# A third place for x in the shared-expert stage, earlier loads and gathers, and constant rows by a transfer in attention

## The chip, the cores and the metric

One core of a Trainium2 chip runs the whole program: TensorE (PE), VectorE (DVE), ScalarE (ACT), GpSimd (POOL) and SyncE (SP), which only issues transfers here. The metric is the device time in microseconds, the median of three runs. SP's transfers go through one hardware queue, those that POOL issues (gathers and scatters by an index) through another.

## The reference, cut to what matters

```python
x = x + long_convolution(ctx, layernorm(x))      # 2048 tokens of 512
x = x + bitlinear_ffn(layernorm(x))
x = x + cross_attention(layernorm(x), ctx)       # 16 heads, 8 batches of 256 tokens
h = layernorm(x)                                 # the layer that the change is in:
aff = sigmoid(h @ wa)                            # 16 routed experts
topk_p, topk_i = top_k(aff, 2)                   # 2 experts a token, shares normalised
routed = sum over the two of share * expert(h)
shared = expert_s0(h) + expert_s1(h)             # 2 experts that every token takes
x = x + h + shared + routed
# expert(h) = (gelu(h @ g + gb) * (h @ w1 + b1)) @ w2 + b2,   512 -> 256 -> 512
```

## The kernel before, in words

The program is a sequence of blocks, and all engines meet at the end of each. Three of them matter.

**Attention** (`stage_attention`) goes through steps (b, u): batch b of 8, pair u of heads of 8, one step being g = 8b + u. Each engine has its list of work written out for every step. PE transposes scores with a stationary operand `kb[b % 2]`: 96 rows of keys and 32 constant rows of which two are ones and the rest zeros. The constant rows of `kb[0]` are made in the block before. Those of `kb[1]` (`at_kb`) are made at step (0, 2) by two memsets on DVE (L1577, L1579), and the output bias is split there too into a high and a low bf16 part (L1582, L1584). PE needs the constant rows at g = 8 and the bias at step (2, 0). DVE's copies of the turned maxima (`qs`, L1590) stand behind all this in its queue, and PE's `transposed_scores` (L1678) waits for them.

**Router** (`stage_router`) is untouched by the change. It leaves x + h in HBM, called x below (`mid_rows`, 16 tiles of 128 tokens).

**Route and shared** (`stage_route_and_shared`) does two things at once. PE runs the two shared experts over six chunks i of 256 tokens (CN = 6): `up(i, 0)`, `down(i - 1)`, `up(i, 1)`, where an `up` is 24 matmuls into `ps_sg` and 24 into `ps_su`. DVE adds each `down` to x (`add_sums`, L2186), which frees the banks that the next `down` needs. x for chunk i lies in one of two places: `s_x` for even i, `e_yo` for odd i. SP loads it (`load_x`, L2079) and stores the sum back (`store_x`, L2083). Beside this, the 32 weight matrices of the routed experts (512 KB each, number n) are loaded in order by SP (`load_raw`, L2074), rounded to bf16 by ACT (L2296), and the rest is subtracted out by POOL for even n (`gate_lows`, L2136) and by DVE for odd n (`up_lows`, L2179). A load waits until the matrix that had its place is done with. SP's queue is in order, so that a load of x stands behind the loads of weights that are ahead of it in the list. The list gives chunk i the weights `LOADS[i]`: 7 to 9, 10 to 13, 14 to 19, 20 to 25, 26 to 29, 30 and 31. Numbers 28, 29 and 30 wait for `up_lows(10)`, `gate_lows(11)` and `up_lows(11)`, and 31 waits for `gate_lows(14)`.

The routing itself: DVE works out a slot for each token and share. POOL scatters 32 pieces into a table in HBM (L2140), four between two `gate_lows`, and SP loads the finished table (`s_table`, L2104) behind weight 29. PE turns it (`turn_table`, L2360) between `down(4)` and `up(5, 1)`. DVE makes of it the token numbers of 47 blocks, and POOL gathers the rows of the first two blocks into `e_rows` (L2154). This is the last thing in POOL's list, behind `gate_lows(15)`.

**Experts** (`stage_experts`) runs the 47 blocks of 128 slots and then the shared experts for the last two chunks. Its first matmuls (`ps_ex`, L2640) turn the rows gathered above, then come `ps_eg` and `ps_eu`.

## Time and profile before

| | before |
|---|---|
| median of 3 runs | 1229.19 us (1228.75 to 1229.37) |
| the profiled execution | 1229.41 us, its span 1227.5 us |
| PE busy, weight loads | 1076.3 us (88%), 807.1 us (66%) |
| DVE, ACT, POOL busy | 896.5 us, 715.6 us, 600.0 us |
| mean granted clock of TensorE | 0.929 of 2.4 GHz |
| mean transfer rate | 151 GB/s |

The span runs from the first to the last instruction. Around it lie 1.9 us. PE is busy most of the time, but no engine is so all the time, since the blocks differ: what an edit is worth shows in the place where it stands.

### The profile page before, as it was taken

Reading aid. Unit: us, or ns where it says so; the run is one execution under the profiler, and the core shown is the slowest. Engines: PE = TensorE matmul, PEld = TensorE weight load, DVE = VectorE, ACT = ScalarE, POOL = GpSimd, SP = SyncE. Lnnn points to the kernel's source line nnn. Section 1 sums busy time; section 2 is a strip of 40 time slices with the busy share of each in tenths; the row PEclk is TensorE's granted clock in tenths of the full one; section 3 lists DMA queues with packets and bytes.
Section 4 is the critical chain, followed back from the end, with each engine's and each line's share of the span. In section 5 each row is a group of like instructions: output and inputs, shape, how many; then the busy total and the mean of one; then the engine's idle time right before and its main releaser. Section 6 shows DMA issues by size and latency. Waiting matters only on the chain. (4 is left out here: it accounts for less than half of the span.)

```text
span 1227.5 us, 25636 instructions
## 1 busy us (share of the span) xinstructions
PE 1076.3 (88%) x9595; PEld 807.1 (66%) x9691; DVE 896.5 (73%) x1671; ACT 715.6 (58%) x1090; POOL 600.0 (49%) x586
## 2 busy tenths in 40 slices
PE   5799996768999799967899998698988599999995
PEld 4677775734554567736777776397756488888883
DVE  6389998977888798667788888488845555555538
ACT  4475772758888555646788877295533255544530
POOL 1444441635455322336788888322686255555520
PEclk9899998879999999968999999857989899999998
DMA  7484431033333312321222220098588377677789
GB/s 278 144 269 128 155 106 60 7 112 121 120 103 125 116 34 95 96 87 27 53 55 58 59 58 11 13 385 295 131 240 249 129 238 239 240 242 242 236 308 366
DMA packets 77872, 185.03 MB, mean 151 GB/s; under 512 B 10032, under 2 KB 12230, under 8 KB 76860
## 3 DMA queue, kind: packets, MB, share of 16 engines
q1 hardware_dynamic: 61468, 139.92, 34.0%
q0 software_dynamic: 8544, 24.68, 6.6%
q10 hardware_dynamic: 7744, 18.88, 5.1%
q8 instruction: 74, 1.21, 0.5%
q14 instruction: 42, 0.34, 0.1%
HBM read 130.06 MB, written 47.09 MB: 144 GB/s over the span
## 5 line engine op out<-in xcount | busy, mean ns | idle before, releaser
L384 PE MATMUL ps_y<-kv,toep 128*128 128x288 f32 x640 | 159.1, 411 | 6.7 <-POOL kv L368 6.0
L384 PEld LDWEIGHTS ps_y<-kv,toep 128*128 128x128 f32 x640 | 122.4, 192 | 42.8 <-DMA toep<-taps_padded 8.5
L1489 POOL TENSOR_TENSOR vw<-at_pf,kw 128x1024 bf16<-128x1024 f32 x64 | 136.5, 2133 | 2.7 <-ACT kw L1546 2.7
L368 POOL TENSOR_TENSOR kv<-kx 128x1024 f32<-128x1024 f32 x32 | 60.6, 1893 | 87.9 <-PE ps_y L384 38.3
L2443 POOL DMA_INDIRECT expert_results<-e_yo,target x47 | 70.1, 1492 | 56.9 <-ACT e_yo L2486 56.9
L1542 ACT ACTIVATE at_pf<-ps_st 128x1024 f32<-128x1024 f32 x64 | 65.4, 1022 | 46.4 <-PE ps_st L1678 43.0
L1596 DVE TENSOR_REDUCE at_negmax<-ps_s 128x4 f32<-128x1024 f32 x64 | 78.4, 1224 | 2.8 <-PE ps_s L1639 0.8
L999 PEld LDWEIGHTS ps_eg<-e_xT,e_w 128*128 128x128 bf16 x1128 | 67.8, 99 | 14.6 <-issue 2.5
L2540 DVE COPY e_w<-expert_weights 128x4096 bf16 x47 | 57.7, 1227 | 23.6 <-issue 23.6
L999 PE MATMUL ps_eg<-e_xT,e_w 128*128 128x128 bf16 x1128 | 71.9, 221 | 3.4 <-DVE e_xT L2547 3.4
L940 PE MATMUL ps_fH<-w1T,f_qaT 128*128 128x512 bf16 x253 | 62.3, 402 | 9.9 <-ACT f_h L835 8.8
L999 PE MATMUL ps_eu<-e_xT,e_w 128*128 128x128 bf16 x1128 | 70.9, 219 | 0.0
L1546 ACT ACTIVATE kw<-at_pf 128x1024 bf16<-128x1024 f32 x64 | 67.7, 1057 | 2.0
L2553 DVE SCALAR_TENSOR_TENSOR e_y<-ps_eu,e_bias,e_y 128x128 f32<-128x128 f32 x94 | 28.6, 346 | 54.0 <-PE ps_eu L999 53.2
L2438 POOL DMA_INDIRECT e_rows<-token_rows,token x45 | 43.5, 967 | 48.7 <-PE ps_ex L2640 42.6
L999 PEld LDWEIGHTS ps_eu<-e_xT,e_w 128*128 128x128 bf16 x1128 | 65.3, 98 | 0.0
L2502 ACT ACTIVATE e_xT<-ps_ex 128x512 bf16<-128x512 bf16 x47 | 28.1, 597 | 63.7 <-PE ps_ex L2640 63.7
L1590 DVE COPY qs<-ps_m 32x256 bf16<-32x256 bf16 x128 | 37.6, 294 | 33.9 <-PE ps_m L1651 30.8
L408 DVE TENSOR_TENSOR prod<-ps_y,qx 128x1024 f32<-128x1024 f32 x32 | 39.1, 1223 | 29.2 <-ACT ps_y L337 29.1
L964 PE MATMUL ps_fY<-w2T,f_qbT 128*128 128x512 bf16 x242 | 57.4, 387 | 2.4 <-DVE x_res L773 1.7
L940 PEld LDWEIGHTS ps_fH<-w1T,f_qaT 128*128 128x128 bf16 x256 | 25.9, 103 | 42.3 <-issue 15.2
L2495 ACT ACTIVATE e_y<-ps_eg,e_bias 128x128 f32<-128x128 f32 x94 | 29.4, 363 | 37.9 <-PE ps_eg L999 29.7
(446 smaller groups left out, 3164.1 us busy)
## 6 DMA issues: line engine op xcount, KB each, us to landing
e_parts<-down_parts SPq DMA_DIRECT2D x47, 512.0 KB
w_raw<-in_L_ffn_w ACTq DMA_DIRECT2D x32, 512.0 KB, 4.8
toep<-taps_padded SPq DMA_DIRECT2D x32, 256.0 KB, 3.5
f_draw<-in_L_ffn_rw SPq DMA_DIRECT2D x16, 512.0 KB
down_parts<-f_dparts SPq DMA_DIRECT2D x16, 512.0 KB
expert_weights<-expert_results SPq DMA_DIRECT2D x16, 512.0 KB, 11.0
x_res<-in_x SPq DMA_DIRECT2D x4, 1024.0 KB, 11.8
c_in<-in_ctx SPq DMA_DIRECT2D x4, 1024.0 KB, 7.8
```

What stands on the lines that cost most here:

```text
L368: pool.tensor_tensor(pairs[:, :, :, 0:HD0], x[:, :, 0:HD0].unsqueeze(2).broadcast_to([P, ROWS_N, WIDE, HD0]), partners(x, 0, 1, WIDE), ALU ...
L384: last = pe.matmul(y[:, l * B:(l + 1) * B, :, WIDE - 1:], toep[h % 2][:, (DC - 1 - l + m) * P:(DC - l + m) * P], kv[h % 2][:, m * B:(m + 1 ...
L940: pe.matmul(psH[:, f, :], qaT[p][:, c, :], k.w1T[:, c * FF + f * 512:c * FF + (f + 1) * 512], start=(c == 0), stop=False)
L964: last = pe.matmul(psY[:, :], qbT[p][:, c, :], k.w2T[:, c * D:(c + 1) * D], start=(c == 0), stop=(c == FC - 1))
L999: instruction = pe.matmul(out, stationary[a], moving[b], start=first and n == 0, stop=last and n == 2)
L1489: pool.tensor_tensor(pl[u % 4][:, :, :, :], pf[u % 2][:, :, :, :], ph[u % 4][:, :, :, :], ALU.subtract)\
L1542: act.activation(pf[u % 2][:, :, :, :], psT[:, :, :, :], ACT.Exp, scale=SCORE_SCALE).then_inc(exped, 1)
L1546: act.activation(ph[u % 4][:, :, :, :], pf[u % 2][:, :, :, :], ACT.Copy).then_inc(p_high, 1)
L1596: dve.tensor_reduce(negmax[u % 2][:, :].rearrange("p (j q) -> p j q", j=2), psS[:, :, :, :], AX.X, ALU.max, negate=True).then_inc(max_read, 1)
L2438: pool.indirect_dma_start(out=rows[j % 2], out_offset=None, in_=k.scratch["rows"], in_offset=bass.IndirectOffsetOnAxis(ap=token[:, j:j + 1 ...
L2443: pool.indirect_dma_start(out=k.scratch["results"], out_offset=bass.IndirectOffsetOnAxis(ap=target[:, j:j + 1], axis=0), in_=yo[j % 2], in ...
L2540: dve.tensor_copy(w1[j % 2][:, :, :, :].rearrange("p h c f -> p (h c f)"), W[:, bass.ds(e, 1), :, :, :].rearrange("p o h c f -> p (o h c f ...
```

## The change

In the shared stage x has three places instead of two: `s_x`, `e_yo` and `e_rows` (the target of the later gathers), used in the order 0, 1, 2, 0, 2, 1. Each load has a semaphore for its place and half. The loads of chunks 0 to 2 are issued together near the start, that of chunk 3 ahead of weight 20, that of chunk 4 behind weight 29 and ahead of the table, and that of chunk 5 ahead of weight 30. A load into a used place waits for the store out of it, and each store waits for the store before it. PE turns the slot table between the two halves of the last `up`. POOL issues the two gathers ahead of `gate_lows(15)`, and each waits for the store of chunk 4 out of `e_rows`. In attention a transfer on SP copies the constant rows of `kb[0]` to `kb[1]` at the start of the block. The two memsets go, and the bias is split at step (1, 5).

```diff
@@ -1411,7 +1411,7 @@
             sem(n) for n in ("xn", "xtp", "xh", "xl", "qp", "sq", "no", "qh", "ql"))
         sum_psum, var_ready, r_ready, diag_ready, r_psum = (sem(n) for n in ("sup", "var", "rr", "di", "rp"))
         ot_psum, ot_high, ot_low, y_psum, y_added = (sem(n) for n in ("otp", "oth", "otl", "yp", "ya"))
-        maxes_high, ones_set, bias_zeroed, bias_high, bias_low, shift_ready = (sem(n) for n in ("mxh", "os", "bz", "bh", "bw", "xs"))
+        maxes_high, ones_copied, bias_zeroed, bias_high, bias_low, shift_ready = (sem(n) for n in ("mxh", "oc", "bz", "bh", "bw", "xs"))
         stacked, k_loaded = sem("st"), sem("kl")
         block = ctx.enter_context(nc.Block())
         G = UNITS
@@ -1433,6 +1433,7 @@
 
         @block.sync
         def _(sp):
+            sp.dma_start(kb[1][STACK:, :, :, :], kb[0][STACK:, :, :, :]).then_inc(ones_copied, 16)
             sp.wait_ge(bias_zeroed, 1)
             for row in (0, LO_ROW):
                 sp.dma_start(bo[row:row + 1, :], k.ins["L1_xattn_bo"].rearrange("(o d) -> o d", o=1)).then_inc(b_loaded, 16)
@@ -1573,10 +1574,7 @@
 
             for b, u in STEPS:
                 g = b * G + u
-                if b == 0 and u == 2:
-                    dve.memset(kb[1][STACK:, :, :, :], 0.0).then_inc(ones_set, 1)
-                    dve.wait_ge(ones_set, 1)
-                    dve.memset(kb[1][STACK:STACK + 2, :, :, :], 1.0).then_inc(ones_set, 1)
+                if b == 1 and u == 5:
                     lo_row = slice(LO_ROW, LO_ROW + 1)
                     dve.wait_ge(b_loaded, 32)
                     dve.tensor_copy(bo_parts[:, :], bo[:, :]).then_inc(bias_high, 1)
@@ -1671,7 +1669,7 @@
                 if g:
                     pe.wait_ge(exped, g)
                 if g == G:
-                    pe.wait_ge(ones_set, 2)
+                    pe.wait_ge(ones_copied, 16)
                 c, h0 = u // 2, 2 * (u % 2)
                 for j in range(2):
                     for kc in range(2):
@@ -1801,6 +1799,7 @@
 RAW_N = OWN_RAW + LENT_RAW
 SETS = 4
 LO_AT = 32
+X_PLACE = (0, 1, 2, 0, 2, 1)
 HI_AT = 64
 FRONT = 4
 K_ROWS = 96
@@ -2049,14 +2048,16 @@
         table_set, table_stored, table_loaded, table_turned = (sem(n) for n in ("tse", "tst", "tl", "tt"))
         cols_set, cols_ready, cols_turned, shares_ready, token_ready, rows_got = (sem(n) for n in ("cs", "cr", "ctn", "shr", "tok", "brow"))
         raw_loaded, raw_high, gate_low, up_low = [sem(f"rl{i}") for i in range(RAW_N + LENT_RAW)], sem("rh"), sem("gl"), sem("ul")
-        xT_loaded, x_loaded = ([sem(f"{n}{i}") for i in range(2)] for n in ("xtl", "xl"))
+        xT_loaded = [sem(f"xtl{i}") for i in range(2)]
+        x_loaded = [[sem(f"xl{i}{s}") for s in range(ST)] for i in range(max(X_PLACE) + 1)]
         block = ctx.enter_context(nc.Block())
         turned_dram = k.scratch["turned"].rearrange("(i s) p d -> i p s d", s=ST)
         mid_dram = k.scratch["mid"].rearrange("(t p) d -> t p d", p=P)
         table_dram = k.scratch["slots"]
         W_half = lambda n, h: W[:, n // 2, h, :, n % 2 * FE:(n % 2 + 1) * FE]
         rows_loaded, x_stored, late_loaded = fetched
-        x_tile = lambda i, s: e_yo[s] if i % 2 else x[:, s, :]
+        x_tile = lambda i, s: (x[:, s, :], e_yo[s], e_rows[s].bitcast(F32))[X_PLACE[i]]
+        x_uses = lambda i: [n for n in range(i + 1) if X_PLACE[n] == X_PLACE[i]]
         experts_of = lambda i: range(FIRST_E[i], FIRST_E[i + 1])
         shares_of = lambda tile: late_shares[0:K_ROWS, tile - ST * LATE[0], :] if tile // ST in LATE else (
             sharesT[0:K_ROWS, tile if tile < ST * LATE[0] else tile - 2 * ST, :])
@@ -2074,12 +2075,14 @@
                 sp.dma_start(raw_at(n), src).then_inc(raw_loaded[place_of(n)], 16)
 
             def load_x(i, s):
-                if i >= 2:
-                    sp.wait_ge(x_stored[s], 16 * (i - 1))
-                sp.dma_start(x_tile(i, s), mid_dram[EARLY[i] * ST + s, :, :]).then_inc(x_loaded[s], 16)
+                if len(x_uses(i)) > 1:
+                    sp.wait_ge(x_stored[s], 16 * (x_uses(i)[-2] + 1))
+                sp.dma_start(x_tile(i, s), mid_dram[EARLY[i] * ST + s, :, :]).then_inc(x_loaded[X_PLACE[i]][s], 16)
 
             def store_x(i, s):
                 sp.wait_ge(d_added, i * ST + s + 1)
+                if i:
+                    sp.wait_ge(x_stored[s], 16 * i)
                 sp.dma_start(mid_dram[EARLY[i] * ST + s, :, :], x_tile(i, s)).then_inc(x_stored[s], 16)
 
             for n in range(RAW_N):
@@ -2088,22 +2091,24 @@
             sp.dma_start(table_dram.rearrange("(j p) w -> j p w", p=BLK), table[:, :, :]).then_inc(table_stored, 16)
             sp.dma_start(bias_rows[0:E_N, 0:FE], k.ins["L1_ffn_rgb"]).then_inc(rows_got, 16)
             sp.dma_start(bias_rows[0:E_N, FE:], k.ins["L1_ffn_rb1"]).then_inc(rows_got, 16)
-            for s in range(ST):
-                load_x(0, s)
+            for i in range(3):
+                for s in range(ST):
+                    load_x(i, s)
             for i in range(CN):
-                for s in range(ST):
-                    if i >= 2:
-                        load_x(i - 1, s)
+                if i in (3, 5):
+                    for s in range(ST):
+                        load_x(i, s)
                 for n in LOADS[i]:
                     load_raw(n)
                     if n == LOADS[i][0] and i >= 2:
                         for s in range(ST):
                             store_x(i - 2, s)
+                if i == 4:
+                    for s in range(ST):
+                        load_x(i, s)
                 if i == CN - 2:
                     sp.wait_ge(scattered, 16 * 2 * NT)
                     sp.dma_start(table[:, :, :], table_dram.rearrange("(j p) w -> j p w", p=BLK)).then_inc(table_loaded, 16)
-            for s in range(ST):
-                load_x(CN - 1, s)
             for s in range(ST):
                 store_x(CN - 2, s)
             sp.wait_ge(gu_psum, (CN - 1) * SH_N)
@@ -2147,12 +2152,15 @@
             for e in range(2, E_N):
                 for n in range((e - 2) * 4, min((e - 1) * 4, 2 * NT)):
                     scatter(n)
-                gate_lows(e)
+                if e < E_N - 1:
+                    gate_lows(e)
             pool.wait_ge(scattered, 16 * 2 * NT)
             pool.wait_ge(token_ready, 1)
             for j in range(2):
+                pool.wait_ge(x_stored[j], 16 * (CN - 1))
                 pool.indirect_dma_start(out=e_rows[j], out_offset=None, in_=k.scratch["rows"],
                                         in_offset=bass.IndirectOffsetOnAxis(ap=token[:, j:j + 1], axis=0)).then_inc(rows_loaded[j], 16)
+            gate_lows(E_N - 1)
 
         @block.vector
         def _(dve):
@@ -2182,7 +2190,7 @@
             def add_sums(i):
                 for s in range(ST):
                     dve.wait_ge(d_psum, i * ST + (s + 1))
-                    dve.wait_ge(x_loaded[s], 16 * (i + 1))
+                    dve.wait_ge(x_loaded[X_PLACE[i]][s], 16 * len(x_uses(i)))
                     dve.tensor_tensor(x_tile(i, s), x_tile(i, s), psD[s][:, :], ALU.add).then_inc(d_added, 1)
 
             for t in range(NT):
@@ -2323,6 +2331,8 @@
         def _(pe):
             def up(i, p, e):
                 for ps, m in ((psG, 0), (psU, 1)):
+                    if m and i == CN - 1 and e == SH_N - 1:
+                        turn_table()
                     for f in range(F2):
                         for c in range(DC):
                             col = c * FE + f * P
@@ -2373,8 +2383,6 @@
                 pe.wait_ge(y_full, i * SH_N - 1)
                 up(i, i % 2, 0)
                 down(i - 1)
-                if i == CN - 1:
-                    turn_table()
                 pe.wait_ge(y_full, i * SH_N)
                 up(i, i % 2, 1)
             down(CN - 1)
```

## Rows read from the trace of the kernel before

**Rows 1.** Timeline, attention, 549 to 560 us: start, duration, engine, line, operation, [idle before it].

```profile
...
550.32 1.76 DVE L1577 MEMSET at_kb<- 32x2048 uint32 x1 [0.48 <-issue]
...
551.65 1.09 PE L1689 MATMUL ps_p<-ident,at_xn 128*128 128x128 f32 x4
...
552.99 3.47 DVE L1579 MEMSET at_kb<- 2x4096 bf16 x1 [0.91 <-DVE at_kb L1577]
556.49 0.42 DVE L1582 CAST at_bop<-at_bo 33x512 bf16<-33x512 f32 x1
556.95 0.68 DVE L1584 TENSOR_TENSOR at_bop<-at_bo,at_bop 1x512 bf16<-1x512 f32 x1
...
558.33 1.03 PE L1678 MATMUL ps_st<-qs,kb 128*128 128x256 bf16 x4 [5.58 <-DVE qs L1590]
```

**Rows 2.** Timeline of DVE, attention, around the step (1, 5).

```profile
...
596.66 0.62 DVE L1590 COPY qs<-ps_m 32x256 bf16<-32x256 bf16 x2 [2.71 <-PE ps_m L1651]
```

**Rows 3.** Timeline of DVE, shared stage: adds of x, and the stage's last one.

```profile
...
913.81 1.28 DVE L2186 TENSOR_TENSOR s_x<-s_x,ps_sd 128x512 f32<-128x512 f32 x2 [9.95 <-DMA s_x<-mid_rows]
...
932.83 1.29 DVE L2186 TENSOR_TENSOR e_yo<-e_yo,ps_sd 128x512 f32<-128x512 f32 x2 [8.14 <-DMA e_yo<-mid_rows]
...
957.94 1.27 DVE L2186 TENSOR_TENSOR e_yo<-e_yo,ps_sd 128x512 f32<-128x512 f32 x2
```

**Rows 4.** Timeline of PE, shared stage from 892 us on.

```profile
...
892.87 0.60 PE L2339 MATMUL ps_sd<-down_bias,s_sharesT 96*128 96x512 bf16 x2
...
898.48 2.78 PE L999 MATMUL ps_sg<-s_xT,sgu 128*128 128x256 bf16 x24
...
914.55 1.20 PE L2339 MATMUL ps_sd<-down_bias,s_sharesT 96*128 96x512 bf16 x2 [5.43 <-DVE s_x L2186]
...
923.08 2.78 PE L999 MATMUL ps_sg<-s_xT,sgu 128*128 128x256 bf16 x24
...
942.85 0.43 PE L2360 MATMUL ps_stab<-ident,s_table 47*128 47x47 f32 x2 [3.10 <-DMA s_table<-slot_table]
943.22 4.41 PE L999 MATMUL ps_sg<-s_xT,sgu 128*128 128x256 bf16 x24
...
950.13 0.60 PE L2339 MATMUL ps_sd<-down_bias,s_sharesT 96*128 96x512 bf16 x2
...
956.26 0.38 PE L999 MATMUL ps_sd<-sd,s_ylo 128*128 128x512 bf16 x1
```

**Rows 5.** Stretches: busy (x count) of PE, PEld, DVE, ACT, POOL; clock, DMA share, GB/s.

```profile
...
914.00:920.00 6.00, 5.23 (x12) 1.90 (x14) 5.36 (x9) 3.25 (x5) 4.95 (x5) 0.50 1.11 211
...
961.00:963.00 2.00, 0.00 (x0) 0.00 (x0) 0.00 (x0) 0.00 (x0) 0.00 (x0) 0.56 1.02 387
```

**Rows 6.** Timeline of SP's queue, shared stage.

```profile
...
907.25 0.91 SPq L2079 DMA_DIRECT2D s_x<-mid_rows  x2
...
921.29 0.33 SPq L2074 DMA_DIRECT2D s_raw<-in_L_ffn_rw  x1
...
936.91 0.29 SPq L2104 DMA_DIRECT2D s_table<-slot_table  x1
```

**Rows 7.** Timeline of POOL, end of the shared stage and after.

```profile
...
931.19 2.12 POOL L2136 TENSOR_TENSOR expert_weights<-s_raw,expert_weights 128x1024 bf16<-128x1024 f32 x1
...
957.09 1.80 POOL L2154 DMA_INDIRECT e_rows<-token_rows,token  x1 [0.15 <-issue]
959.19 0.95 POOL L2154 DMA_INDIRECT e_rows<-token_rows,token  x1 [0.30 <-issue]
965.67 0.15 POOL L2446 IOTA e_places<- 128x1 f32 x1 [5.53 <-POOLq L1980]
```

**Rows 8.** DMA issues in 922 to 926 us: queue, count, KB, us to landing.

```profile
...
expert_weights<-in_L_ffn_rg SPq DMA_DIRECT2D x2, 512.0 KB, 8.8
```

**Rows 9.** The chain that ended last: start, duration, group.

```profile
...
968.41 2.72 PE ps_eg L999 x24
...
980.53 1.34 PE ps_eg L999 x24
```

## The prediction

> **What bounds the kernel now.** I read the page first. No engine is full over the whole span, so I looked for places where PE waits, with the list of waits, the timeline of PE, and, for each wait, the timelines of the engine or queue that ended it. The change touches three such places.
>
> In attention PE stands for 5.58 us ahead of a transposed score, and DVE, for which it waits, makes constants in that time [rows 1]. In the shared stage PE waits 5.43 us for an add of x, and the add had waited 9.95 us for a load that SP had issued at 907.25, only 6.6 us before [rows 3, 4, 6]. It waits 3.10 us for the slot table [rows 4]. After the last `down` (956.6) nothing runs on PE until 965.7, and POOL is the last to be busy before the engines meet [rows 4, 7]. Each of these gaps is followed by matmuls at half speed: the granted clock is 0.50 from 914 to 920, which is the lower level, 1.2 GHz, and 0.56 around 962, after 4 us and more without a matmul [rows 5].
>
> **Attention.** The change removes two memsets, 1.76 and 3.47 us, and the 0.91 us between them. It moves the two bias operations, 0.42 and 0.68 us [rows 1]. From the first memset to the end of the bias split DVE spends 7.3 us (550.32 to 557.63). With these gone, the copy of the maxima is ready as soon as PE has turned them, and PE becomes the limit: it is busy with turning x until 551.65 + 1.09 = 552.7, so that the score that now starts at 558.33 starts at about 552.6. That is 5.7 us. Below it, the bound is 4.5 us, if something of the chain between DVE and POOL is late by a microsecond. Above it, 7.3 us, all that DVE spent. I take 5.8. All engines go through the steps of attention in lockstep, so it stays.
>
> The moved bias operations cost 1.1 us at step (1, 5). DVE waits there 2.71 us for PE [rows 2], which covers them. Without this cover they would cost 1.1. The transfer of the constant rows is one issue on SP at the start, about 0.4 us ahead of the loads of bias and keys, and 256 KB to move. No row has a transfer within SBUF. The nearest, 512 KB from HBM in a crowded time, landed after 8.8 us [rows 8]. It is issued some 12 us before the memsets now stand and is needed some 20 us after them. The cost is nothing, and at the upper bound, 8.8 us from issue to landing, still nothing.
>
> **Shared stage, the waits for x.** With three places x for chunk 2 is there from the start, so that the wait of 5.43 us goes. An undisturbed `down` takes 898.48 - 892.87 = 5.6 us, and the one after the wait took 923.08 - 914.55 = 8.5 us [rows 4], at the lower clock [rows 5]. Together 8.3 us: PE is through `down(3)` at 914.7 instead of 923.1. The load of chunk 3 takes the queue position of the old load for chunk 2 (907.25), lands about 6.6 us later, and its add is not due until about 918. The wait of 8.14 us at 932.83 [rows 3] goes too. The four x loads that are issued sooner are the same bytes in another order. They stand behind the first weights, in a time when the next weights wait for their places, and I cost them at nothing (1 us at most).
>
> What is late next? Two things take most of the 8.3 us back. Weight 23 is issued at 921.3 [rows 6], because its place is freed by POOL, which alternates between scatters and subtractions and doesn't gain from the change. At 7 to 8.8 us to landing [rows 8], ACT rounds it, and only then the hidden layer of (4, 1), at 929 to 932. `down(4)`, now begun at about 925, stands in its middle for 1 to 4 us. And the table load stands behind weight 29, which waits for POOL's `gate_lows(11)`. That operation begins at 931.19 and ends at 933.3 [rows 7], in an unbroken row of work, and the change leaves it there. So the table load moves only from 936.9 to about 934.7: 933.3, then the issue of the weight and of two x loads, 1.3 us. It takes now 942.85 - 936.91 = 5.9 us to PE [rows 4, 6]. With 4.5 to 6 us PE can turn it at 939.2 to 940.7, and I take 940. PE arrives at the middle of `up(5, 1)` between 935 and 938, and waits there 2 to 5 us. The move of the turn into the `up` only puts 2.8 us of matmuls ahead of the wait. The half behind it takes 2.8 us, or 4.4 at the lower clock, as its sister took at 943.22 [rows 4]; it ends at about 944.5 (between 942.5 and 946). Today `up(5, 1)` ends at 950.1. Of 8.3 us some 5.6 are left here.
>
> **Shared stage, the end.** Today 950.1 is followed at 959.5 by the last store, and the last `gate_lows` and both gathers stand in a row. The second gather is issued until 960.1, and the engines go on at 965.7, which is 5.5 us later [rows 7]. The DMA engines are full around 962 [rows 5], so I read this as the block's end waiting until the gathered rows have landed. The row can't tell that from a fixed cost after POOL's last instruction (a rival). Now the gathers move ahead of `gate_lows(15)`, but each waits for the store of chunk 4, since they overwrite its place. That store waits in turn for the store of chunk 3, which SP issues behind weight 30 at about 936.5. If a store takes as long as a load of x, 6.6 us, chunk 3's is through at 943. Chunk 4's add is done by then (its load is issued with the table), and its store is through at about 948 (5 to 6.6 us later: 948 to 949.6; 946.5 if the queue is emptier). The token numbers are ready before that. The two gathers take 960.14 - 957.09 = 3.05 us, and 5.5 us more to the meeting: 956.6, with bounds of 955.0 and 958.2. `gate_lows(15)`, 2.1 us, lies inside. Queued behind the waiting gathers there is only it, and nobody waits for it but the block's end.
>
> The other way to the end goes by PE: 944.5, and 959.5 - 950.1 = 9.4 us from there to the last store, so 953.9. It is shorter, so the gathers decide. The experts begin at 956.6 instead of 965.7: 9.1 us.
>
> The Trainium skill speaks against this term (SBUF — State Buffer, section "Who interferes with whom"): POOL builds the descriptors of its own DMAs through a port pair that it shares with DVE, and is blocked while some DVE operations hold it. The rows have one gather issue of 0.95 us and one of 1.80 us [rows 7]. If both took 1.8 us or more among DVE's work, 1 us would be added, and if one waited through several operations, more; it is a rival below. The 1.80 us stand beside DVE work, which fits the rule and doesn't show it.
>
> **Start of the experts.** The first 24 matmuls take 2.72 us, later ones 1.34 [rows 9], because the clock fell during the gap. The gap shrinks from 9 to about 6 us. That may or may not save it: 0 to 2 us, I take 0.7. The Trainium skill's TensorE: Matmul & The Clock Gate, "What's actually happening", has the low clock as the default which activity lifts. By it nothing is saved, since the gap stays several microseconds long, and the sum would be 0.7 us smaller. The trace agrees as to the 9 us gap; of a 6 us gap it shows that of 5.43 us, after which the clock was 0.50 too [rows 4, 5].
>
> **Sum.** 5.8 + 9.1 + 0.7 = 15.6 us. The profiled execution took 1229.41 us, so it would be 1213.8. The median of the runs is 0.2 us lower: 1213.6.
>
> **Rivals.** (A) The meeting is not tied to the gathers' landing but comes 5.5 us after POOL's last instruction. That is now `gate_lows(15)`, which ends 2.2 us after the gathers: 1215.8. For it: rows 7 can't exclude it. (B) The stores of x are quicker, and the end goes by PE: experts at 953.9 to 955, so 1211.5; with the table a microsecond earlier too, 1210. (C) POOL's descriptors are held up by DVE, or the queue in front of the table is slower (the new wait of chunk 4's load for the store of chunk 2 stands ahead of the table load, and weights took 8.8 us in that time). Each microsecond shows in full: 2 to 5 us, 1216 to 1219. (D) The edit in attention brings little, because POOL's chain of maxima or the clock takes the time: 1217 to 1219. (E) Slower than before: the transfer of constant rows within SBUF is slow. It has about 32 us until PE needs it, and decides from there on, 1 us for 1 us. It would have to take 32 + 15.6 = 48 us for no gain, 52 for 1233, which is 5 GB/s for 256 KB. Against it is every transfer in these rows.
>
> **How the numbers follow.** Forecast 0.48, A 0.14, B 0.16, C 0.11, D 0.07, E 0.02, and 0.02 for a gain that I can't see lost otherwise. The forecast's own spread is 1211.5 to 1216. The range takes in A and B whole and the nearer half of C and D: 1209 to 1219. A difference under 0.2%, 2.5 us, is no change for this kernel. Faster 0.96, same 0.02, slower 0.02.
>
> **What the profile after should show.** No memset on `at_kb`, and the score of step 3 right behind PE's turn of x, with a wait of less than 1 us. In the shared stage no wait of DVE for x in chunks 2 and 3. A wait of PE for the table of 2 to 5 us inside `up(5, 1)`, in the middle, with the table's load issued near 934.7 less the 5.8 of attention. Gathers ahead of POOL's last subtraction, and the gap on PE ahead of `ps_ex` at 5 to 6 us. What would make me wrong: a POOL queue that is faster or slower than now, or a gap at the end that doesn't shrink.

## The result, and the profile after

The change takes 1223.81 us (median of 20 runs, 1219.57 to 1231.66) beside 1231.67 us for the kernel before, measured on the same chips (20 runs, 1228.75 to 1240.38). The ratio is 0.9934, with a 95% interval of 0.9914 to 0.9954, so the gain is 8.1 us (5.7 to 10.6). The prediction had 15.6 us. The profiled execution took 1225.11 us, its span is 1223.4 us. One of the 29 executions of the kernel before that ran beside the first four experiments took 2191.51 us and is in no ratio.

The engines meet at the end of each block of the program. The trace has these meetings, and from one to the next the profiled executions took, in us:

| kernel | attention | route and shared | experts |
|---|---|---|---|
| before | 254.9 | 124.4 | 261.9 |
| the change | 248.9 | 121.5 | 264.6 |
| attention_only | 255.2 | 121.8 | 264.6 |
| shared_only | 254.8 | 118.9 | 264.6 |
| pool_yields | 248.0 | 117.2 | 261.9 |
| gathers_last | 248.8 | 124.4 | 262.3 |
| warm_boundary | 248.0 | 121.4 | 262.2 |
| yields_and_warm | 248.0 | 119.4 | 261.1 |
| turn_at_old_place | 248.0 | 119.2 | 264.7 |
| pool_yields_later | 248.0 | 117.6 | 261.9 |
| yields_and_queue | 248.0 | 116.1 | 265.2 |
| third_place_alone | 248.0 | 125.4 | 264.8 |

Rows with the same code in a block show how far one execution can be trusted: the block of route and shared took 124.4 and 121.8 us with the old code (before, attention_only) and 121.5, 118.9 and 121.4 with the new (the change, shared_only, warm_boundary). The experts, whose code only the two runs with added matmuls touch, lie at 261.1 to 262.3 or at 264.6 to 265.2. So a difference of up to 2.8 us in one block is read only together with the medians or with a row that shows its cause. For the new code one cause stands in the rows of POOL: its 32 scatters took 36.0 us together in shared_only, 37.8 in the change and 37.6 in warm_boundary, and what stands behind them in its list starts later by as much.

**Attention.** The timeline of PE in the change, at the step before the one of the memsets and at that step itself, which waited 5.58 us [rows 1] (start, duration, operation, [idle before it]):

```profile
550.48 1.03 PE L1676 MATMUL ps_st<-qs,kb 128*128 128x256 bf16 x4 [0.71 <-DVE qs L1588]
...
554.38 0.63 PE L1676 MATMUL ps_st<-qs,kb 128*128 128x256 bf16 x4
```

The wait of 5.58 us is gone, and nothing of it is left at its step. The 0.71 us of the step before stood there in the kernel before too. The block is 6.0 us shorter. The transfer that replaces the memsets, `at_kb<-kb`, took 12.5 us from issue to landing:

```profile
at_kb<-kb SPq DMA_DIRECT2D x1, 256.0 KB, 12.5
```

That is above the 8.8 us taken as its bound, and still nothing waits for it. The two bias operations, at their new step, in the timeline of DVE, and below them what POOL did beside the second:

```profile
589.80 0.41 DVE L1580 CAST at_bop<-at_bo 33x512 bf16<-33x512 f32 x1
590.25 2.65 DVE L1582 TENSOR_TENSOR at_bop<-at_bo,at_bop 1x512 bf16<-1x512 f32 x1
592.93 0.62 DVE L1588 COPY qs<-ps_m 32x256 bf16<-32x256 bf16 x2
```

```profile
590.23 2.12 POOL L1490 TENSOR_TENSOR vw<-at_pf,kw 128x1024 bf16<-128x1024 f32 x1
```

The second took 2.65 us for a single row of 512, where it had taken 0.68 with POOL idle beside it [rows 1]. It ended 0.55 us behind POOL's subtraction. The cover of 2.71 us [rows 2] is used up: the copy behind it has no wait left. This is the first sign of what follows.

**Shared stage.** The four adds of x for chunks 2 to 5 in the change have no wait at all [rows 3]; the prediction had said so for chunks 2 and 3. But here is the timeline of PE (compare [rows 4]):

```profile
921.01 0.60 PE L2349 MATMUL ps_sd<-down_bias,s_sharesT 96*128 96x512 bf16 x2
...
935.75 1.04 PE L999 MATMUL ps_sd<-sd,s_yhi 128*128 128x512 bf16 x2 [11.56 <-DVE s_ylo L2179]
...
943.22 0.44 PE L2370 MATMUL ps_stab<-ident,s_table 47*128 47x47 f32 x2
...
958.80 1.02 PE L2648 MATMUL ps_ex<-ident_b,e_rows 128*128 128x128 bf16 x8 [6.08 <-PEq L1979]
```

PE stands for 11.56 us in the middle of `down(4)`, for DVE's low part of the second expert's hidden layer. Now DVE and POOL at this time, one timeline each:

```profile
922.64 1.22 DVE L2187 TENSOR_TENSOR expert_weights<-s_raw,expert_weights 128x1024 bf16<-128x1024 f32 x1
925.68 10.01 DVE L2179 TENSOR_TENSOR s_ylo<-s_gf,s_yhi 128x512 bf16<-128x512 f32 x1 [1.83 <-ACT s_yhi L2326]
935.62 0.86 DVE L2172 SCALAR_TENSOR_TENSOR s_gf<-ps_su,vectors,s_gf 128x256 f32<-128x256 f32 x2
```

```profile
924.72 4.20 POOL L2141 TENSOR_TENSOR expert_weights<-expert_weights 128x1024 bf16<-128x1024 f32 x2
928.87 2.11 POOL L2141 TENSOR_TENSOR expert_weights<-s_raw,expert_weights 128x1024 bf16<-128x1024 f32 x1
930.96 4.19 POOL L2141 TENSOR_TENSOR expert_weights<-expert_weights 128x1024 bf16<-128x1024 f32 x2
```

The reader is to see that DVE did not wait for an input. It had started at 925.68, and what takes 0.68 us alone took 10.01. POOL began a row of five subtractions at 924.72, one of them close behind another, and ended it at 935.15; DVE's instruction ended 0.54 us later. The kernel before already had the two kinds of instruction side by side, where they cost little. This is from its timelines, DVE first and then POOL, rows that the prediction did not use:

```profile
915.80 1.21 DVE L2179 TENSOR_TENSOR expert_weights<-expert_weights 128x1024 bf16<-128x1024 f32 x1
...
919.04 3.31 DVE L2179 TENSOR_TENSOR expert_weights<-expert_weights 128x1024 bf16<-128x1024 f32 x1
...
935.95 0.69 DVE L2171 TENSOR_TENSOR s_ylo<-s_gf,s_yhi 128x512 bf16<-128x512 f32 x1
```

```profile
919.13 2.13 POOL L2136 TENSOR_TENSOR expert_weights<-s_raw,expert_weights 128x1024 bf16<-128x1024 f32 x1
...
927.02 4.21 POOL L2136 TENSOR_TENSOR expert_weights<-expert_weights 128x1024 bf16<-128x1024 f32 x2
...
936.60 2.13 POOL L2136 TENSOR_TENSOR expert_weights<-expert_weights 128x1024 bf16<-128x1024 f32 x1 [3.28 <-ACT expert_weights L2296]
```

DVE's subtraction takes 1.21 us alone and 3.31, longer by POOL's 2.1, beside one of POOL's. The low part that `down(4)` needs stood at 935.95, 2.6 us behind the end of POOL's row of three subtractions (933.31, [rows 7]) and in the gap ahead of the next. Told from the block's start, the change moved it from 94.7 to 88.4 us, and the row, now of five, lies from 87.5 to 97.9.

The Trainium skill, SBUF — State Buffer, section "Who interferes with whom", has the rule: a DVE instruction with two SBUF inputs contends with a POOL instruction that reads SBUF, for a port pair that is an exclusive lock. The trace agrees that DVE is held. In the change POOL's row had begun 0.96 us ahead of DVE's instruction; in the pair of 3.31 and 2.13 us the profile has DVE's start 0.09 us ahead of POOL's, and DVE is held all the same. The section speaks of one instruction's length. Here the hold lasted through five.

**The end.** The last rows of POOL, in the change (compare [rows 7]):

```profile
951.15 0.99 POOL L2161 DMA_INDIRECT e_rows<-token_rows,token  x1 [5.66 <-DMA mid_rows<-e_rows]
952.45 1.05 POOL L2161 DMA_INDIRECT e_rows<-token_rows,token  x1 [0.30 <-issue]
953.52 2.13 POOL L2141 TENSOR_TENSOR expert_weights<-s_raw,expert_weights 128x1024 bf16<-128x1024 f32 x1
958.77 0.15 POOL L2454 IOTA e_places<- 128x1 f32 x1 [3.12 <-POOLq L1979]
```

From the end of the second gather's issue to the next block are 958.77 - 953.50 = 5.27 us, before 5.53. From POOL's last instruction they are 3.12, before 5.53. So the gathers brought the meeting forward. Their rows landed earlier than that, 3.4 us behind the issue (the median of the two), so by 957:

```profile
e_rows<-token_rows,token POOLq DMA_INDIRECT x2, 3.4
```

The meeting came about 2 us behind the landing. And as the last subtraction begins 0.02 us behind the second gather, the distance can be told from either.

### The profile page after: what moved, and what is told of

Same layout as the page of the kernel before. It is cut to its first block and busy times, and to the rows that moved or that the text cites. A ratio compares the mean times of both kernels' runs of the same rounds, so it can differ in the third digit from the quotient of the medians.

```text
span 1223.4 us, 25745 instructions
## 1 busy us (share of the span) xinstructions
PE 1080.5 (88%) x9691; PEld 805.7 (66%) x9691; DVE 898.9 (73%) x1669; ACT 715.2 (58%) x1090; POOL 599.4 (49%) x586
## 3 DMA queue, kind: packets, MB, share of 16 engines
q8 instruction: 74, 1.21, 0.4%
## 5 line engine op out<-in xcount | busy, mean ns | idle before, releaser
L368 POOL TENSOR_TENSOR kv<-kx 128x1024 f32<-128x1024 f32 x32 | 60.6, 1893 | 87.5 <-PE ps_y L384 38.0
L1594 DVE TENSOR_REDUCE at_negmax<-ps_s 128x4 f32<-128x1024 f32 x64 | 78.3, 1224 | 2.4 <-PE ps_s L1637 0.5
L940 PE MATMUL ps_fH<-w1T,f_qaT 128*128 128x512 bf16 x256 | 65.1, 411 | 9.1 <-ACT f_h L835 8.4
L1588 DVE COPY qs<-ps_m 32x256 bf16<-32x256 bf16 x128 | 37.6, 294 | 33.0 <-PE ps_m L1649 29.8
L408 DVE TENSOR_TENSOR prod<-ps_y,qx 128x1024 f32<-128x1024 f32 x32 | 39.1, 1223 | 28.8 <-ACT ps_y L337 28.8
L999 PE MATMUL ps_ed<-e_parts,e_yhi 128*128 128x512 bf16 x188 | 55.9, 379 | 0.4 <-DVE e_ylo L2569 0.4
```

Of the source, the lines that this page charges most:

```text
L368: pool.tensor_tensor(pairs[:, :, :, 0:HD0], x[:, :, 0:HD0].unsqueeze(2).broadcast_to([P, ROWS_N, WIDE, HD0]), partners(x, 0, 1, WIDE), ALU ...
L940: pe.matmul(psH[:, f, :], qaT[p][:, c, :], k.w1T[:, c * FF + f * 512:c * FF + (f + 1) * 512], start=(c == 0), stop=False)
L999: instruction = pe.matmul(out, stationary[a], moving[b], start=first and n == 0, stop=last and n == 2)
L1594: dve.tensor_reduce(negmax[u % 2][:, :].rearrange("p (j q) -> p j q", j=2), psS[:, :, :, :], AX.X, ALU.max, negate=True).then_inc(max_read, 1)
```

## The experiments

Each ran beside the kernel before. attention_only, shared_only, pool_yields and gathers_last came first, together.

### attention_only

The kernel before with `stage_attention` of the change, nothing else:

```diff
+sp.dma_start(kb[1][STACK:, :, :, :], kb[0][STACK:, :, :, :]).then_inc(ones_copied, 16)
-if b == 0 and u == 2:
-    dve.memset(kb[1][STACK:, :, :, :], 0.0).then_inc(ones_set, 1)
-    dve.wait_ge(ones_set, 1)
-    dve.memset(kb[1][STACK:STACK + 2, :, :, :], 1.0).then_inc(ones_set, 1)
+if b == 1 and u == 5:
```

> The kernel before with the attention part of the change alone. In the profile after, the attention block is 6.0 us shorter than before (from PE's first score to PE's first work of the router) and the shared block 2.8 us shorter. If the parts simply add, this run is 6.0 us faster than the kernel before, ratio 0.995, and its shared block is as long as before (124.4 us). Rival: the whole gain of the change is in attention and the rest is noise or a loss that shows only in the experts' first blocks; then this run is as fast as the whole change or faster, ratio 0.993 or less.

Measured: 1224.43 us (12 runs), ratio 0.9940 (0.9916 to 0.9963), so 7.4 us (4.6 to 10.4). The wait at the start of attention is gone in its profile as in the change's, yet the block took 255.2 us. The stretch of 30 us in the middle of attention, first of the change and then of this run (busy time of PE, PEld, DVE, ACT, POOL, then the granted clock, DMA share and GB/s):

```profile
620.00:650.00 30.00, 29.46 (x391) 23.69 (x390) 25.15 (x57) 24.74 (x33) 24.14 (x31) 1.00 0.23 58
```

```profile
620.00:650.00 30.00, 28.98 (x374) 22.81 (x375) 23.58 (x52) 23.80 (x31) 23.11 (x28) 0.94 0.22 54
```

The mean clock is 0.94 there, and again in the next three such stretches, where the change has 1.00. PE did 374 matmuls in place of 391. This one execution, at 1232.20 us far above its median, lost in attention by the clock what the edit had brought. The nine other profiled executions with the new attention have 248.0 to 248.9 us, 6.0 to 6.9 less than before. So neither this profile nor its block is the measure here but the ratio, and it gives the attention edit 7.4 us.

### shared_only

The change with `stage_attention` of before, so the lines above the other way round:

```diff
-if b == 1 and u == 5:
+if b == 0 and u == 2:
+    dve.memset(kb[1][STACK:, :, :, :], 0.0).then_inc(ones_set, 1)
...
```

> The changed kernel with the attention of before. If the parts add, the ratio is 0.998 to 1.000: 2.8 us less in the shared block, of which the first blocks of the experts take some back (2.7 us in the one profile pair, which I put down to where the clock's fall lies). The operation of DVE on the low part of the hidden layer (4, 1) takes about 10 us again, as in the profile after, if POOL's row of subtractions holds it; it takes 0.7 us if that was an accident of one execution.

Measured: 1230.46 us, ratio 0.9980 (0.9956 to 1.0005): 2.5 us, and possibly none. DVE's low part took 10.45 us and PE stood 9.73 us in `down(4)`, so the hold does not come from attention or from a shift in time. The two halves add up to 9.9 us, with intervals that hold the change's 8.1.

### pool_yields

GpSimd waits, once, before `gate_lows(10)` (the tenth low part if the first is number 0) until VectorE's two low parts of chunk 4 are made (`YIELD = 10`). Of the row of five subtractions one stands before the wait and four behind it:

```diff
 def gate_lows(e):
     pool.wait_ge(raw_high, 2 * e + 1)
+    if e == YIELD:
+        pool.wait_ge(y_low, 4 * SH_N + 2)
     pool.tensor_tensor(W_half(2 * e, 1), ...)
```

> The changed kernel with one wait more: POOL's subtraction for expert 10 waits until DVE has made the low part of (4, 1). Theory (port): in the profile after this DVE operation took 10.0 us instead of 0.7 because five subtractions of POOL stood back to back beside it; with the wait it takes under 3 us, PE's wait of 11.6 us inside down(4) shrinks to 3 to 4 us, POOL loses about 1 us, and the experts start 3 to 6 us sooner: ratio against before 0.988 to 0.991. Rival (transfers): DVE is slow there because the DMA engines are full in that time (401 GB/s); then it stays at about 10 us and POOL, now waiting for it, makes everything behind it later: slower than the change by 3 us or more. Rival (table): PE is released sooner and only waits longer for the slot table; the experts start within 1 us of the changed kernel.

Measured: 1217.31 us (6 runs, 1216.32 to 1220.26), ratio 0.9871 (0.9842 to 0.9899). That is 15.9 us below before, and 6.5 us below the change by the medians. A wait more made the kernel faster. The timelines of DVE, POOL and PE:

```profile
925.56 0.68 DVE L2182 TENSOR_TENSOR s_ylo<-s_gf,s_yhi 128x512 bf16<-128x512 f32 x1
```

```profile
926.39 2.12 POOL L2144 TENSOR_TENSOR expert_weights<-expert_weights 128x1024 bf16<-128x1024 f32 x1 [1.84 <-DVE s_ylo L2182]
```

```profile
926.30 1.03 PE L999 MATMUL ps_sd<-sd,s_yhi 128*128 128x512 bf16 x2 [3.17 <-DVE s_ylo L2182]
...
937.85 0.44 PE L2373 MATMUL ps_stab<-ident,s_table 47*128 47x47 f32 x2 [3.28 <-DMA s_table<-slot_table]
...
953.47 1.01 PE L2651 MATMUL ps_ex<-ident_b,e_rows 128*128 128x128 bf16 x8 [4.45 <-PEq L1980]
```

The low part takes 0.68 us, the wait in `down(4)` is 3.17 us, inside the 1 to 4 that the prediction had, and the wait for the table is 3.28, inside its 2 to 5. The expected rival, by which full DMA engines slow DVE down, is refuted: from 924 to 927 us they were as full (share 1.12, 360 GB/s; in the change 1.05 and 401 from 925 to 930), and the low part took 0.68.

By the block alone POOL's wait is worth 4.3 us (121.5 to 117.2), in which POOL's scatters, 36.6 us in this execution and 37.8 in the change, have a part of up to 1.2. The experts' 2.7 us between the two profiles are the clock, which falls once or twice with and without this wait (see warm_boundary).

### pool_yields_later

The same with `YIELD = 12`, so that three of POOL's five subtractions stand before the wait and two behind it. It was tried after gathers_last, and belongs here.

> GpSimd's wait two subtractions later, before the twelfth low part instead of the tenth. Theory: VectorE's low part of the middle of down(4) is held as long as GpSimd's subtractions follow one another without a gap, and ends with the last of them before the wait. Three of them (6.3 us) begin about 1 us before it, so it takes 5 to 6 us, where it took 10.0 with five of them and 0.7 with none. TensorE stands 6.5 to 8 us inside down(4) instead of 11.6 and 3.2; of the 4 to 5 us between this and the earlier wait 3.3 are taken from TensorE's wait for the table, so the block is 118 to 119 us long and the run takes 1218 to 1219.5. Rival: only one instruction of GpSimd is waited out and then the port is given to VectorE, and what helped was another effect of the wait: the low part takes 2 to 3 us, or stays at 10.

Measured: 1218.96 us (1216.87 to 1225.52), ratio 0.9903 (0.9881 to 0.9924), and:

```profile
924.13 6.04 DVE L2182 TENSOR_TENSOR s_ylo<-s_gf,s_yhi 128x512 bf16<-128x512 f32 x1 [1.65 <-ACT s_yhi L2329]
```

```profile
923.34 4.20 POOL L2144 TENSOR_TENSOR expert_weights<-expert_weights 128x1024 bf16<-128x1024 f32 x2
927.50 2.12 POOL L2144 TENSOR_TENSOR expert_weights<-s_raw,expert_weights 128x1024 bf16<-128x1024 f32 x1
930.32 5.19 POOL L2144 TENSOR_TENSOR expert_weights<-expert_weights 128x1024 bf16<-128x1024 f32 x2 [0.71 <-DVE s_ylo L2182]
```

POOL's first three end at 929.62, and DVE's low part at 930.17, 0.55 us behind. With no, three and five of POOL's subtractions in a row it took 0.68, 6.04 and 10.01 us. PE's wait in `down(4)` was 7.26 us. The hold lasts to the end of POOL's row and not for one instruction; the rival is refuted. The block took 117.6 us, only 0.4 more than in pool_yields: of the 4.1 us that PE stood longer, 3.28 are its wait for the table, which is gone.

### gathers_last

The change with the two gathers again behind POOL's last subtraction:

```diff
-                if e < E_N - 1:
-                    gate_lows(e)
+                gate_lows(e)
...
-            gate_lows(E_N - 1)
```

> The changed kernel with the two gathers behind POOL's last subtraction again. Theory (the block's end waits for the gathered rows): the subtraction ends at about 951.6 of the profile after, the gathers are issued until 954.7 and the block ends 5.5 us later, at 960.2 instead of 958.7: 1 to 2.5 us slower than the change. Rival (the end comes a fixed time after POOL's last instruction, 3.1 us in the profile after): the block ends at 957.8, so 1 us faster than the change.

Measured: 1227.08 us, ratio 0.9953 (0.9924 to 0.9981). The block took 124.4 us, 2.9 more than in the change, and the medians differ by 3.3, both more than the 1 to 2.5 expected. The meeting moved with the gathers:

```profile
957.09 0.95 POOL L2160 DMA_INDIRECT e_rows<-token_rows,token  x1 [0.31 <-issue]
963.52 0.15 POOL L2452 IOTA e_places<- 128x1 f32 x1 [5.49 <-POOLq L1979]
```

It comes 5.48 us behind the second issue, which is last in POOL's list again. In the change the same distance is 5.27 and POOL's last instruction lies in it. The rival's 3.1 us behind POOL's last instruction, whichever that is, are refuted.

That the gathers themselves set the meeting isn't shown by this. In seven of the eight profiled executions in which a subtraction is last, the meeting comes 3.12 or 3.13 us behind that subtraction (in the eighth, yields_and_warm, PE had come last); in the four in which a gather is last, 5.48 to 5.76 us behind the gather. turn_at_old_place parts the two readings: its last subtraction began 0.43 us behind the second gather and took 2.47 us, and the meeting came 6.03 us behind the gather and 3.13 behind the subtraction. So the time seems to hang on what POOL did last. SP's last store was issued 0.51 us before that meeting, so this one execution doesn't settle it.

### turn_at_old_place

pool_yields, with `turn_table()` back between `down(4)` and `up(5, 1)`:

```diff
-                    if m and i == CN - 1 and e == SH_N - 1:
-                        turn_table()
...
                 down(i - 1)
+                if i == CN - 1:
+                    turn_table()
```

> GpSimd's wait kept, and turn_table() back at its old place, between down(4) and up(5, 1). Theory: the table is there at about 937.8 us of that trace, wherever TensorE waits for it; in the trace with GpSimd's wait TensorE stood 3.3 us inside up(5, 1), behind the 2.6 us of its gate product. Back at the old place these 2.6 us come behind the table: the wait is 5.9 us, the shared block about 2.6 us longer (119.8 instead of 117.2), the run 1219.5 to 1220.5. The path by the gathers doesn't lose it, since the token numbers come from the table and not from the product: if the end of the block follows the gathers and chunk 4's stores alone, and these wait for nothing of up(5, 1), the run stays at 1217.3 (rival).

Measured: 1221.25 us (1219.16 to 1224.79), ratio 0.9918 (0.9901 to 0.9935). PE waits 7.83 us for the table in place of 3.28, and the block took 119.2 us, 2.0 more. The medians differ by 3.9. So the moved turn is worth 2 to 4 us, and the rival, by which it would be worth nothing, is refuted. Of the 2.0 us the gathers carry over half: the second one's issue ended 113.1 us after the block's start (948.82 - 835.7), in pool_yields 112.0. The rest lies behind it, where POOL's last subtraction began later and took 2.47 us instead of 2.13.

### third_place_alone

pool_yields with the gathers last and the turn at its old place, so that of the shared stage's edits only the third place and the sooner loads are left. Its edit is that of gathers_last and that of turn_at_old_place together, on top of pool_yields.

> Of the shared stage's change only the third place for x with the sooner loads, beside GpSimd's wait before its tenth low part: the gathers stand again behind the last low part and turn_table() between down(4) and up(5, 1). Attention as in the change. Theory: the three parts add up as the runs priced them, 2.9 us for the gathers and 2.0 for the turn on top of the block's 117.2: 122.1 us, which leaves the third place 2.3 us of the 7.2 that the whole brings against 124.4, and the run takes 1221.5 to 1223. Rival 1: the third place brings nothing by itself, since behind it TensorE waits for the table as long as it waited for x: the block takes 124.4 and the run 1224 to 1225. Rival 2: the parts overlap and the third place brings more than half, 119 to 120.5, run 1219.5 to 1221.

Measured: 1229.52 us (12 runs), ratio 0.9951 (0.9926 to 0.9976); the block took 125.4 us. Rival 1 had 124.4 for the block and fits it best; its 1224 to 1225 for the run is missed, with single executions from 1223.48 to 1236.27. The timeline of PE:

```profile
927.53 1.03 PE L999 MATMUL ps_sd<-sd,s_yhi 128*128 128x512 bf16 x2 [2.74 <-DVE s_ylo L2180]
...
939.79 0.47 PE L2369 MATMUL ps_stab<-ident,s_table 47*128 47x47 f32 x2 [8.00 <-DMA s_table<-slot_table]
```

The two waits for x, 8.3 us of PE in the prediction's count, come back as one wait of 8.00 us for the table, and the gathers still stand behind POOL's last subtraction. The three parts don't add: the third place brings nothing by itself (the ratio, 0.9951, is no better than attention_only's 0.9940), and on top of it the moved turn and the moved gathers bring 8 us of the block (125.4 to 117.2). What these two would bring without it was not run.

### yields_and_queue

pool_yields, and in SP's list the table's load right behind weight 28, and the stores of chunk 4 ahead of weight 31 (`RAWS = 32`, `TABLE_AFTER = 28`):

```diff
+if n == RAWS - 1:
+    for s in range(ST): store_x(CN - 2, s)
 load_raw(n)
+if n == TABLE_AFTER:
+    sp.wait_ge(scattered, 16 * 2 * NT)
+    sp.dma_start(table[:, :, :], ...)
```

> GpSimd's wait before its tenth low part kept, and two transfers of SyncE's queue taken out from behind waits: the slot table is loaded right behind the 29th weight load (before the 30th, which waited until 930.6 us in that trace) instead of behind both and the loads of x, and chunk 4's stores are issued before the last weight load (issued at 940.2, waiting for a place) instead of behind it. Theory: the table lands 3 to 5 us sooner, TensorE's wait of 3.3 us inside up(5, 1) goes, chunk 4's stores go out at about 936 to 939 instead of 941.1, the gathers follow them by the 4 us that a store needs and the meeting follows the second gather by 5 to 5.5 us; the block takes 114 to 115 us instead of 117.2, which is what the prediction had taken (115.3), and the run 1214 to 1215.5. Rival: the last product and its sums hold the end: down(5)'s end and the last store bound the block, and it stays at 116.5 to 117, the run at 1217.

Measured: 1217.76 us (1216.62 to 1220.83), ratio 0.9863 (0.9835 to 0.9891), the same as pool_yields. The block took 116.1 us, 1.1 less, of which the medians show nothing. PE still waited 2.80 us for the table: its load could be issued no sooner than 927.90, since SP then waited for the last scatter. It went out 93.7 us after the block's start, in pool_yields 95.7. So SP's order was only part of what made the table late, and the last scatter sets the bound. The lower end, 114 us, was not reached.

### warm_boundary and yields_and_warm

24 matmuls of 512 columns that nobody reads, on PE behind `down(5)`, and six more behind the first block's turns; once on the change and once on pool_yields:

```diff
             down(CN - 1)
+            pe.wait_ge(gelu_done, CN * SH_N)
+            pe.wait_ge(y_full, CN * SH_N)
+            for n in range(24):
+                pe.matmul(psG[n % 2][:, :, :].rearrange("p f t -> p (f t)"), sgu[:, 0, 0, 0, 0:P], sd[:, 0, 0, 0:D], start=True, stop=True)
```

> The change with 24 matmuls of 512 columns that nobody reads on TensorE behind down(5), in the time in which it stands until the shared block's end (6.1 us in the trace of the change), and 6 more behind the first block's turns in the experts. They touch neither the meeting nor the rows. Theory: the experts' stage is 2.8 us longer in the change's trace (264.6 against 261.9) because the granted clock is 0.5 from 1.5 us before its start to 8.7 us behind it and again from 12.2 to 15.6, after TensorE stood; with TensorE busy over the boundary the clock stays at 1.0 or falls for less, the first ps_eg row takes 1.5 us instead of 2.7, the stage takes about 260 us, and the run 1220 to 1222 where the change takes 1224. Rival 1: the length of the stage follows the gathers and the weights, not the clock: the rows take less, the stage stays at 262 to 265 and the run at 1224. Rival 2: the added matmuls delay the first block, by up to 3 us at the low clock: 1225 to 1227.

> The same matmuls on top of GpSimd's wait before its tenth low part (which brought 1217.3). By the theory that the clock lengthens the experts' start: 1214 to 1216. By rival 1: 1217. By rival 2, since TensorE stands there for only 4.5 us before the meeting and 24 matmuls take 5.1 us at the full and 10.2 at the low clock: 1218 to 1222.

Measured: 1221.74 us (1221.35 to 1222.67), ratio 0.9917 (0.9903 to 0.9932) on the change, and 1220.36 us (1217.61 to 1221.73), ratio 0.9899 (0.9882 to 0.9916) on pool_yields. The stretch behind the meeting, in the change and then with the added matmuls:

```profile
961.00:966.00 5.00, 4.49 (x43) 4.52 (x44) 1.94 (x5) 0.00 (x0) 0.67 (x1) 0.50 0.57 196
...
971.00:975.00 4.00, 4.00 (x46) 4.00 (x45) 1.28 (x2) 0.63 (x2) 0.00 (x0) 0.59 0.14 54
```

```profile
961.00:966.00 5.00, 3.59 (x52) 3.28 (x49) 2.32 (x5) 1.30 (x4) 1.72 (x2) 1.00 0.47 125
...
971.00:975.00 4.00, 3.95 (x58) 3.29 (x56) 2.37 (x5) 2.21 (x5) 2.46 (x2) 1.00 0.47 150
```

With PE busy up to the meeting the clock is 1.00 where it was 0.50, which is 2.4 in place of 1.2 GHz, and the experts took 262.2 us in place of 264.6. So the experts' longer time was the clock. The twelve profiles agree: in the six that took 264.6 to 265.2 us the mean granted clock falls again, to 0.57 to 0.73, from 12 to 16 us behind the meeting, and in the six that took 261.1 to 262.3 it is 0.98 to 1.00 there. It is not a cost of the change: attention_only has the old shared stage and also took 264.6. The experts of warm_boundary were no shorter than those of the other executions with a single fall. On pool_yields the added matmuls delayed PE instead: it had 0.30 us of wait left ahead of `ps_ex` (4.45 without them), the block took 2.2 us more, and the run 3 us more, inside rival 2's 1218 to 1222. Of the block's 2.2 us only 0.9 are PE's, by which the meeting came 3.99 us behind POOL's last subtraction in place of 3.12; in this execution POOL's scatters took 39.1 us, in pool_yields 36.6.

## Why the prediction was wrong

**Attention: right.** 5.8 us forecast, 6.0 in the block, 7.4 (4.6 to 10.4) by the run with this part alone. Rivals D and E are refuted. Two covers were thinner than taken: the transfer landed after 12.5 us, and the bias operations took 3.1 us against a cover of 2.71.

**The step that failed** is "`down(4)`, now begun at about 925, stands in its middle for 1 to 4 us", in the shared stage's waits. It measured 11.56 us. The step looked at when the weight would land and ACT be done, which was right (ACT ended at about 925.7), and gave DVE's low part behind it no term. What the runs showed in its place: DVE's low part falls into POOL's unbroken row of subtractions and is held until the row ends. The row was known to the prediction, which used it only for the time of the table's load [rows 7], and the rule was known too. It was weighed only the other way round, for POOL's gathers held by DVE, which they were not (0.99 and 1.05 us). pool_yields takes the hold off the low part. It also puts the rest of POOL's row 1.84 us later, and one hold stays, of DVE's subtraction ahead of the low part (2.95 us instead of 1.22).

**What followed from it,** in us from the start of the block (841.3 before, 837.2 in the change, 836.2 in pool_yields):

| | predicted | change | pool_yields |
|---|---|---|---|
| wait inside `down(4)` | 1 to 4 | 11.56 | 3.17 |
| table's load issued | 93.4 | 95.1 | 95.7 |
| `up(5, 1)` done | 103.2 | 109.0 | 106.3 |
| second gather issued | 109.8 | 116.3 | 112.0 |
| meeting | 115.3 | 121.5 | 117.2 |

Without the hold the block is 1.9 us longer than forecast. With it, 6.2. The gain of the block is 2.9 us instead of 9.1, and with POOL's wait 7.2. The table's load went out 1.7 to 2.3 us later than forecast. Here a second, smaller step failed: that the change leaves `gate_lows(11)` where it is. It ended 92.0 us after the block's start before, 93.7 in the change, where the scatters ahead of it took 37.8 us instead of 36.1, and 94.4 in pool_yields, where POOL's wait stands ahead of it. In shared_only the scatters took 36.0, and the load went out at 93.3 as forecast. What makes a scatter take 0.95 us or up to 1.97 was not tried. Rival C had the two engines the other way round, POOL held by DVE, in another place, and priced it at 2 to 5 us. The time of the change lies above its 1219 too.

**The end: right by its number.** The second gather was followed by the meeting after 5.27 us, 5.5 forecast, and rival A's 5.5 us behind POOL's last subtraction were 3.12. The reading behind it, that the block waits for the gathered rows to land, is not borne out (they landed about 2 us or more before); that the time runs from POOL's last instruction, as rival A has it, but is shorter behind a subtraction, fits every execution but the one that PE ended. Rival B did not come up.

**Start of the experts: wrong sign in the profile.** Forecast was a gain of 0.7 us, the block took 2.7 more. By warm_boundary this is the clock, and by attention_only it comes without the change as well. As a term it is noise of the size of 2.8 us, and should have stood as such in the range.

Of the 7.5 us between the forecast gain and the measured one, pool_yields gives back 6.5 by the medians, of which its profile shows 4.3 in the block. That is the main cause, shown. The rest is within the scatter of the runs. That pool_yields comes out at 15.9 us, so near the forecast's 15.6, is in part luck: its block gained 7.2 where 9.1 were forecast, and attention more than its 5.8. What makes the experts' clock fall once or twice in different executions of one kernel stays open.

## What to carry to other kernels

When an edit moves an instruction in time, look not only at what feeds it but at what the other engines run beside it at its new place. Look in the old trace for instructions of the same shape with two durations (here 1.21 and 3.31 us): such a pair showed here what the new schedule would step into for longer. And a wait put on the engine that holds the other up, at the point where the other is on the path, can bring more than it costs: 6.5 us here, where the shared stage's own edits had brought 2.5.

## What was not expected of the hardware

- DVE's instruction was held through three and five consecutive instructions of POOL (6.04 and 10.01 us instead of 0.68), never let in between two of them, and ended 0.54 and 0.55 us behind the last.
- Even a subtraction of a single row of 512 elements was held: 2.65 us instead of 0.68.
- Two executions of the same attention code differed by 6.3 us in that block (255.2 in attention_only, 248.9 in the change), with a granted clock of 0.94 against 1.00 in four stretches of 30 us.
- From POOL's last instruction to the next block it was 3.12 or 3.13 us in seven executions where a subtraction was last, and 5.48 to 5.76 in four where a gather was.
